# A fused attention and ternary-MLP kernel: the first batch normalised by VectorE, half of the first keys issued by ScalarE, epsilon added by GpSimd

## What is computed

```python
x = x + jnp.tanh(g_xattn[0]) * xattn(_layernorm(x), ctx_512, ctx_512)     # 32 query heads, 8 key/value heads, D = 16
x = x + jnp.tanh(g_ffn[0]) * ffn(_layernorm(x), w_gate, w_up, w_down)

def _layernorm(x, eps=1e-05):
    return (x - mean(x)) / sqrt(var(x) + eps)

def h_bitlinear(x, w):                      # ternary weights, 8-bit activations
    xq = act_quant(fwht(x))                 # Walsh-Hadamard transform, then rounding per token
    return xq @ weight_quant(w).T

def ffn(h):
    return h_bitlinear(silu(h_bitlinear(h, w_gate)) * h_bitlinear(h, w_up), w_down)
```

## Time and profile before

| | us |
|---|---|
| median of 3 runs | 474.78 |
| lowest, highest | 474.51, 475.0 |
| the profiled execution, its own time | 474.27 |
| its span in the trace | 472.5 |
| what lies around the span | 1.77 |

### The profile page before, as it was taken

One profiled execution on the slowest core, in us unless ns is written; L12 is line 12 of the kernel. 1 busy time (PEld: TensorE's weight loads), 2 busy tenths in 40 slices (PEclk: granted clock), 3 DMA queues, 4 the chain that ended last, 5 costly groups with the idle time before them and its releaser, 6 DMA issues.

```text
span 472.5 us, 9016 instructions
## 1 busy us (share of the span) xinstructions
PE 458.6 (97%) x3130; PEld 298.9 (63%) x3130; DVE 391.0 (83%) x745; ACT 292.8 (62%) x465; POOL 211.8 (45%) x314
## 2 busy tenths in 40 slices
PE   8999999999999989999999999999999999999997
PEld 7665656566656534468944469864468874479664
DVE  4889998888977759859998967999895999889892
ACT  4478886667777688877647417643616663647460
POOL 4245455989888464655006734202916300930000
PEclk9999999999999999999999999999999999999999
DMA  7999120121014050000100651100361110153086
GB/s 223 323 348 347 45 53 12 24 58 25 13 22 112 13 166 36 1 1 13 24 11 1 112 135 32 22 11 0 67 141 61 24 24 0 28 92 61 1 140 217
DMA packets 68183, 35.90 MB, mean 76 GB/s; under 512 B 50288, under 2 KB 62960, under 8 KB 68144
## 3 DMA queue, kind: packets, MB, share of 16 engines
q1 hardware_dynamic: 67728, 34.61, 28.8%
q10 hardware_dynamic: 416, 0.79, 0.5%
HBM read 19.26 MB, written 4.19 MB: 50 GB/s over the span
## 4 chain that ended last, share of the span: by engine, by line
PE 70%; DVE 13%; issue 7%; ACT 4%; POOL 2%; DMA 1%; SPq 1%; DVEq 0%; POOLq 0%; ACTq 0%
PE ps L863 15%; PE ps L619 10%; PE ps L917 9%; PE ps L602 8%; PE ps L662 6%; PE ps L940 6%; PE ps L679 3%; PE ps L929 2%; PE ps L931 2%; PE ps L806 2%; DVE wst L1447 2%; ACT wst L1052 2%; DVE y_split L1422 2%; PE ps L716 1%; PE ps L627 1%
## 5 line engine op out<-in xcount | busy, mean ns | idle before, releaser
L863 PE MATMUL ps<-wst 128*128 128x512 bf16 x512 | 113.0, 379 | 2.1 <-DVE wst L1442 2.1
L1279 DVE TENSOR_REDUCE reg<-ps 128x4 f32<-128x512 f32 x128 | 81.9, 684 | 24.7 <-PE ps L619 24.0
L863 PEld LDWEIGHTS ps<-wst 128*128 128x128 bf16 x512 | 49.0, 98 | 62.2 <-DVE wst L1442 4.2
L619 PE MATMUL ps<-reg 32*128 32x256 f32 x512 | 86.7, 400 | 0.9 <-DMA reg<-in_k_t 0.5
L1014 ACT ACTIVATE reg<-ps 128x1024 f32<-128x1024 f32 x64 | 65.6, 1025 | 32.8 <-PE ps L627 32.5
L564 POOL TENSOR_TENSOR reg_rest<-reg_rest,z_sc 128x1024 f32<-128x1024 f32 x24 | 47.3, 2012 | 84.6 <-DVE z_sc L1484 84.6
L1146 ACT ACTIVATE wst<-wst 128x512 f32<-128x512 f32 x64 | 40.0, 627 | 51.8 <-DVE wst L1442 51.5
L917 PE MATMUL ps<-had_f,wst 128*128 128x128 f32 x512 | 67.1, 276 | 1.1 <-DVE wst L1447 1.1
L917 PEld LDWEIGHTS ps<-had_f,wst 128*128 128x128 f32 x512 | 64.1, 191 | 4.4 <-DVE wst L1447 1.8
L602 PE MATMUL ps<-reg 32*128 32x512 f32 x232 | 65.2, 639 | 0.0
L619 PEld LDWEIGHTS ps<-reg 32*128 32x128 f32 x512 | 58.7, 184 | 5.8 <-ACT reg L1036 1.0
(11 more groups left out here) (168 smaller groups left out, 738.1 us busy)
## 6 DMA issues: line engine op xcount, KB each, us to landing
wst<-in_w SPq DMA_DIRECT2D x16, 512.0 KB, 8.6
reg<-in_w SPq DMA_DIRECT2D x8, 512.0 KB, 5.6
out<-x_all SPq DMA_DIRECT2D x16, 256.0 KB, 2.1
x_all<-in_x SPq DMA_DIRECT2D x3, 1024.0 KB, 9.5
reg<-in_k_t SPq DMA_DIRECT2D x32, 32.0 KB, 2.4
reg<-in_v SPq DMA_DIRECT2D x4, 256.0 KB, 4.1
x_all<-in_x ACTq DMA_DIRECT2D x1, 512.0 KB, 4.8
reg_rest<-reg SPq DMA_TRANSPOSE x20, 3.0
```

What stands on the lines that cost most here:

```text
L619: last = pe.matmul(ps[:, row_banks(r) + m, 256 * g:256 * g + 256], q_t[n % 4][strip(i), P * h:P * h + P], kpad[n // CHUNK % 2][strip(i), n ...
L863: last = pe.matmul(ps[:, banks[ob % n], :], tern_gu[:, ob // 2, m, j, P * (ob % 2):P * (ob % 2) + P], q1_t[:, j, :], start=(j == 0), stop= ...
L1279: dve.tensor_reduce(neg_max[n % 2][:, g:g + 2, i + m, :], ps[:, row_banks(r) + m, :].rearrange("p (g a t) -> p g a t", g=2, a=2), AX_X, AL ...
```

## The change

It has three parts, and some bookkeeping.

1. The first batch is normalised by VectorE: `first_queries` adds epsilon, waits for GpSimd's power (`first_rsqrt`, which forms no `shift` for batch 0), and does subtract and multiply in one instruction with the strided read of `x_all`. ACT's `normalise_q(0)` goes. In VectorE's queue this stands ahead of `selectors` and `statistics_q(1)`.
2. The first keys of heads 4 to 7 are asked for by ACT, behind batch 1; SP asks for heads 0 to 3 only.
3. For all other batches epsilon is added by GpSimd: `statistics_q` and `statistics` end with `bn_aggr`, and `rsqrt_q`, `front_scale` and `front_scales` begin with a `tensor_scalar` add and a wait for its result.

The bookkeeping: the statistics buffer is doubled, small tiles are views of one tile `few`, semaphore counts follow, one of 16 `spin` calls at the start goes, and PE waits for `identb_set` and `sel_set` only where it first uses those tiles.

```diff
-            load_keys(0)
+            load_keys(0, range(NKV // 2))
@@ GpSimd
-            def rsqrt(n, ready, done, par): ...
+            def first_rsqrt():
+                pool.wait_ge(sem("ve_first"), 1)
+                pool.tensor_tensor(rstd[:, 0:1], ve[:, 0:1], mhalf[:, :], ALU.pow).then_inc(sem("rs_first"), 1)
 def rsqrt_q(n):
-                pool.wait_ge(sem("ve_done"), n + 1)
-                reach(pool, sem("qn_done"), min(n - 1, 4))
+                pool.wait_ge(sem("mv_done"), n + 1)
+                if n == 2:
+                    pool.wait_ge(sem("qn_first"), 1)
+                elif n > 2:
+                    pool.wait_ge(sem("qn_done"), min(n - 2, 3))
                 reach(pool, sem("qp_done"), n - 5)
+                pool.tensor_scalar(ve[:, par:par + 1], mv[:, par, 1:2], EPS, None, ALU.add).then_inc(sem("ve_done"), 1)
+                pool.wait_ge(sem("ve_done"), n)
 def front_scale(tb):
-                rsqrt(Index(None, tb), "f_ve", "f_rs", 2)
                 pool.wait_ge(sem("f_mv"), tb + 1)
+                pool.tensor_scalar(ve[:, 2:3], mv[:, 2, 1:2], EPS, None, ALU.add).then_inc(sem("f_ve"), 1)
+                pool.wait_ge(sem("f_ve"), tb + 1)
+                pool.tensor_tensor(rstd[:, 2:3], ve[:, 2:3], mhalf[:, :], ALU.pow).then_inc(sem("f_rs"), 1)
 def front_scales(u):
+                reach(pool, sem("f_mv"), u.times(UB, UB))
+                pool.tensor_scalar(ve[:, 2:2 + UB], mv[:, 2:2 + UB, 1], EPS, None, ALU.add).then_inc(sem("f_ve"), UB)
                 reach(pool, sem("f_ve"), u.times(UB, UB))
@@ PE
-            spin(16)
+            spin(15)
             pe.wait_ge(sem("ident_in"), 16)
-            pe.wait_ge(sem("identb_set"), 1)
-            pe.wait_ge(sem("sel_set"), 2)
@@ ScalarE
             act.dma_start(x_all[:, 1, :], x[1]).then_inc(sem("x_one"), 16)
+            act.wait_ge(sem("k_zero"), 1)
+            for kv in range(NKV // 2, NKV):
+                i = kv % 4
+                act.dma_start(kpad[0][32 * i + D:32 * i + 2 * D, :, 1, :],
+                              k_t.rearrange("(d k) (b t) -> k d b t", k=NKV, b=NB)[kv, :, 0:CHUNK, :]
+                              ).then_inc(sem("k_in0"), 16)
...
-            normalise_q(0)
@@ VectorE
 def statistics(n, par):
+                reach(dve, sem("f_mv"), n.times(1, -1))
+                dve.bn_stats(st_f[:, n.const % 2, :], x_all[:, n.times(1), :]).then_inc(sem("f_bn"), 1)
                 reach_apart(dve, sem("tanh_done"), (sem("f_bn"), n.times(1, 1)))
+                dve.bn_aggr(mv[:, par, :], st_f[:, n.const % 2, :]).then_inc(sem("f_mv"), 1)
-                dve.wait_ge(sem(names[1]), n.times(1, 1))
-                dve.tensor_scalar(ve[:, par:par + 1], mv[:, par, 1:2], EPS, None, ALU.add).then_inc(sem(names[2]), 1)
+            def first_queries():
+                dve.wait_ge(sem("mv_done"), 1)
+                dve.tensor_scalar(ve[:, 0:1], mv[:, 0, 1:2], EPS, None, ALU.add).then_inc(sem("ve_first"), 1)
+                dve.wait_ge(sem("rs_first"), 1)
+                dve.tensor_scalar(q_norm[0].rearrange("p (m a d) -> p m a d", a=2, d=D),
+                                  x_all[:, 0, :].rearrange("p (d a m) -> p m a d", d=D, a=2),
+                                  mv[:, 0, 0:1], rstd[:, 0:1], ALU.subtract, ALU.mult).then_inc(sem("qn_first"), 1)
...
             statistics_q(0)
+            first_queries()
             selectors()
             statistics_q(1)
```

More of the change, by code:

```diff
@@ L168, in flamingo_block @@
         t8m = sb("t8m", [P, T8], F32)
-        st = sb("st", [P, 6], F32)
         mv = sb("mv", [P, 2 + UB, 2], F32)
@@ L173, in flamingo_block @@
         shift = sb("shift", [P, 2 + UB], F32)
-        mhalf = sb("mhalf", [P, 1], F32)
         r_sum = sb("r_sum", [P, 2, HALF], F32)
-        tg = sb("tg", [P, 2], F32)
-        graw = sb("graw", [P, 2], F32)
-        part = sb("part", [P, 2 * NCH], F32)
[L179 to L184, removed]
+        few = sb("few", [P, 41], F32)
+        tg, graw, mhalf = few[:, 0:2], few[:, 2:4], few[:, 4:5]
+        wsum, wsc, w_inv = few[:, 5:8], few[:, 8:11], few[:, 11:14]
+        wsd_tg, magics = few[:, 14:15], few[:, 15:17]
+        st, st_f = (few[:, k:k + 12].rearrange("p (n k) -> p n k", n=2) for k in (17, 29))
+        m_magic, p_magic = magics[:, 0:1], magics[:, 1:2]
+        part = sb("part", [P, 2 * NCH], F32)
         f_max = sb("f_max", [P, 8], F32)
@@ L268, in _, with load_keys @@
         def _(sp):
-            def load_keys(c):
-                for kv in range(NKV):
+            def load_keys(c, heads=range(NKV)):
+                for kv in heads:
                     i, a = kv % 4, kv // 4
@@ L416, in normalise_q @@
                 par = n % 2
-                pool.wait_ge(sem("sh_done"), n + 1)
+                pool.wait_ge(sem("sh_done"), n)
                 reach(pool, sem("tq_done"), n - 1)
@@ L514, in step @@
                     early_scales(EARLY_HAD[b])
-            rsqrt_q(0)
+            first_rsqrt()
             rsqrt_q(1)
@@ L605, in quarter @@
                         pe.wait_ge(sem("mt_done"), 1)
+                        pe.wait_ge(sem("sel_set"), 2)
                         for m, i in enumerate(own):
@@ L694, in turn_max @@
                 pe.wait_ge(sem("ms"), 5 * n + 5)
+                if n == 0:
+                    pe.wait_ge(sem("identb_set"), 1)
                 if n > 0:
@@ L705, in turn_queries @@
                     return
-                pe.wait_ge(sem("qn_done") if n < 4 else sem("qp_done"), n + 1 if n < 4 else n - 3)
+                if n == 0:
+                    pe.wait_ge(sem("qn_first"), 1)
+                else:
+                    pe.wait_ge(sem("qn_done") if n < 4 else sem("qp_done"), n if n < 4 else n - 3)
                 if n == 3:
@@ L1058, in normalise_q @@
                 par = n % 2
-                act.wait_ge(sem("sh_done"), n + 1)
+                act.wait_ge(sem("sh_done"), n)
                 reach(act, sem("tq_done"), n - 1)
@@ L1238, in selectors, with statistics @@
                     dve.tensor_copy(sel[:, a, :], sel_of[:, a:a + 1].broadcast_to([P, P])).then_inc(sem("sel_set"), 1)
[L1240 to L1244, removed]
-                dve.wait_ge(sem(names[1]), n.times(1, 1))
-                dve.tensor_scalar(ve[:, par:par + 1], mv[:, par, 1:2], EPS, None, ALU.add).then_inc(sem(names[2]), 1)
[L1248 to L1251, removed]
+            def statistics(n, par):
+                reach(dve, sem("f_mv"), n.times(1, -1))
+                dve.bn_stats(st_f[:, n.const % 2, :], x_all[:, n.times(1), :]).then_inc(sem("f_bn"), 1)
+                reach_apart(dve, sem("tanh_done"), (sem("f_bn"), n.times(1, 1)))
+                dve.bn_aggr(mv[:, par, :], st_f[:, n.const % 2, :]).then_inc(sem("f_mv"), 1)
[6 more added lines that the diff above has]
+                                  mv[:, 0, 0:1], rstd[:, 0:1], ALU.subtract, ALU.mult).then_inc(sem("qn_first"), 1)
             def statistics_q(n):
@@ L1262, in statistics_q @@
                 par = n % 2
-                reach(dve, sem("sh_done"), n - 1)
-                dve.bn_stats(st[:, :], x_all[:, n, :]).then_inc(sem("bn_done"), 1)
+                if n == 2:
+                    dve.wait_ge(sem("qn_first"), 1)
+                reach(dve, sem("sh_done"), n - 2)
+                reach(dve, sem("mv_done"), n - 1)
+                dve.bn_stats(st[:, n % 2, :], x_all[:, n, :]).then_inc(sem("bn_done"), 1)
                 dve.wait_ge(sem("bn_done"), n + 1)
-                dve.bn_aggr(mv[:, par, :], st[:, :]).then_inc(sem("mv_done"), 1)
-                dve.wait_ge(sem("mv_done"), n + 1)
-                dve.tensor_scalar(ve[:, par:par + 1], mv[:, par, 1:2], EPS, None, ALU.add).then_inc(sem("ve_done"), 1)
+                dve.bn_aggr(mv[:, par, :], st[:, n % 2, :]).then_inc(sem("mv_done"), 1)
             def maximum(n, k):
@@ L1321, in step @@
                     reach(dve, sem("f_ap"), FRONTS[b])
-                    statistics(Index(None, FRONTS[b]), ("f_bn", "f_mv", "f_ve"), 2)
+                    statistics(Index(None, FRONTS[b]), 2)
             def early_peak(tb):
@@ L1384, in front_statistics @@
                         dve.wait_ge(sem("f_s4"), u.times(2, -2))
-                statistics(n, ("f_bn", "f_mv", "f_ve"), 2 + tb)
+                statistics(n, 2 + tb)
             def input_peak(n, bank=1):
```

2 lines of the change are left out of this document (1 added, 1 removed).

## The result

| | us |
|---|---|
| before, median of 6 runs | 474.70 (474.29 to 475.0) |
| after, median of 6 runs | 472.72 (472.43 to 472.95) |
| ratio, with its 95% interval | 0.9961 (0.9951 to 0.9971) |
| profiled executions, before and after | 474.27 and 472.9 |
| their spans | 472.5 and 471.1 |

The changed kernel is 1.98 us faster; 0.17 was forecast, and the range began at 473.2. A repeat on another chip gave 472.73 against 474.49, 1.76 us less.

What follows compares the result with a forecast made beforehand. PE, busy 458.6 of 472.5 us, was taken to bound the kernel, with a latency at its start. Terms -1.05 + 0.78 - 0.2 + 0.3 = -0.17 us, from the median 474.78, gave 474.6; range 473.2 to 475.7.

Steps and rivals of the forecast that it cites:

- The start: Before PE's first score row: split keys and VectorE's normalisation bring it from 9.71 to 8.66 us, -1.05 us.
- the estimate of 0.9 us: First normalisation: alternative length of VectorE's strided instruction by the page's factor, making the start 0.16 us better.
- What is behind the start: Batch 1's later mean and later-issued batches 2 and 3 stay covered, so PE loses nothing: counted at 0.
- The cover of 0.8 us: Batches 2 and 3: landing at 10.2 us, wanted by VectorE at 11.0, so 0.8 us to spare.
- Rival 2: Batches 2 and 3 land at 13.1 us, VectorE holds row maxima, PE loses 1.4 us: 476.0 us, chance 0.07.
- Steps: Attention steps: GpSimd's added epsilon work makes PE wait 0.39 us at two of four early turns, +0.78 us.
- The lateness of GpSimd: Attention steps: the add and wait in `front_scale` and `rsqrt_q` delay GpSimd by 0.50 us (0.16 + 0.34).
- the forecast's wait at the early turn: PE idle about 0.4 us ahead of L725 in steps 9 and 11, none in 7 and 13.
- a sign of being wrong: Attention steps: the prediction called itself wrong if PE never waits at L725; 0.39 us per wait was forecast.
- End of attention: Two `statistics` and their `ve` instructions in the chain, 0.15 us each, half hidden: -0.2 us for both.
- Boundaries: Two loop boundaries: last `ve` goes (-0.2), GpSimd adds 0.23 and 0.10; +0.15 us each, +0.3 for two.
- Rival 1: GpSimd's addition is hidden, PE doesn't wait at L725, boundaries come out even: 473.5 us, chance 0.26.

Runs made afterwards that it cites:

- s_start: The changed kernel with epsilon added by VectorE for all batches but the first; 471.65 us against 474.21 for the kernel before.
- k_keys: The kernel before with only the first keys split over two queues, SP and ACT; 473.84 us against 474.21 for the kernel before.
- p_split: The changed kernel with one 128x2 VectorE scale instruction in `early_peak` split into two of 128x1; 472.45 us against 474.49 for the kernel before.
- e_steps: The changed kernel with epsilon on GpSimd in the attention steps, on VectorE for the units' scales; 473.61 us against 474.49 for the kernel before.

## Why the prediction was wrong, point by point

**The start, -1.05 forecast.** The mechanism was right: the keys alone moved the first row by 0.47 us (0.44 forecast), both together by 1.25 us in the profiled pair. Two sizes were off. VectorE's strided instruction was taken at 1.06 us by adding GpSimd's penalty for the stride; it takes 0.72, only 0.13 over the contiguous row. Part of that isn't seen, since PE now ends its warm-up matmuls at about 7.1. The Trainium skill's rule of the 16-byte lines (SBUF — State Buffer, Door 1: The DMA port swizzle), weighed there against the move, does little to VectorE in this case (0.13 us), and the estimate of 0.9 us there was too long as well. And one execution's landing of the keys, 9.58 us, was taken for the typical one, though that execution was 0.51 us faster than the median; by the traces that we have this may hide an estimated 0.1 to 0.4 us of the gain (a typical first row at 9.85 or 10.06 in place of 9.71).

**What is behind the start, counted at 0.** Right for after in its amount: its VectorE waits 0.34 us for the third batch, and PE doesn't. The cover of 0.8 us wasn't there, though. ACT issued the transfer at 4.64 us and not at 5.4, but it took 6.6 us and not 4.8. In s_start's trace the wait is 0.68 us, and its lead shrinks from 1.51 to about 0.9 by the first steps. Rival 2 named the mechanism, at the wrong price: where the batch came late enough (k_keys, p_split), PE's idle time was followed by a stretch at half clock, and these executions took 478 to 480 us.

**Steps, +0.78 forecast.** They cost 1.07 us between turns 7 and 11, less 0.33 won before, so 0.74. That this is near 0.78 is luck. The lateness of GpSimd (0.50 forecast, 0.54 at L500 in step 8) was right, and the forecast's wait at the early turn appears in p_split, once. But in the changed kernel PE never waits there, which the prediction had named as a sign of being wrong; 0.71 of the 1.07 us goes through another wait, on VectorE, which the profile of before had already shown: a 128x2 instruction of 0.45 us next to 128x1 ones of 0.15. I read it as a slow instruction and not as a held one. The other 0.36 us is the open part, and the 0.33 won before wasn't forecast.

**End of attention, -0.2 forecast.** -0.42: the `ve` instruction wasn't only half hidden, and VectorE left the chain altogether.

**Boundaries, +0.3 forecast.** -0.52. This is the largest error, 0.8 us, and the step that failed is "each `statistics` gains a wait for the previous aggregate, so its pace stays". The wait is for `f_mv` to reach n - 1, which is the aggregate of two batches back, since the statistics buffer is now double. So the next statistics don't wait, the pace goes from 1.13 to 0.94 us, and four of them give GpSimd more than its add costs. e_steps, with `ve` back on VectorE in the units alone, has the old pace and none of this gain. The forecast also took PE's wait of 0.24 us for granted at both boundaries, and before's timeline has it only at the first.

The sum with the measured terms is -1.25 + 0.74 - 0.42 - 0.52 = -1.45 us, where the spans differ by 1.4; with the means of the first rows (10.06 and 8.38) in place of the pair's it would be -1.9, between the two medians' 1.76 and 1.98. That the keys' landing is what makes up the rest is likely and not shown.

Rival 1 came out nearest in time (473.5), for wrong reasons: GpSimd's addition wasn't hidden, PE paid for it through VectorE.

## What to carry to other kernels

Two latencies that end close together have to be shortened together, and a start that hangs on a transfer has to be read from several executions, not from one. Before an instruction is moved to GpSimd, look at what VectorE does beside GpSimd's long instructions: where, as here, a small VectorE instruction of more than one column takes longer than its like and ends together with a GpSimd one, suspect that it was held, so that a delay of GpSimd becomes a delay of VectorE. When a wait counts a semaphore, work out which instance it names before calling it a dependence on the last one.

## What the runs showed of the hardware that I had not expected

- A VectorE `tensor_scalar` of 128x512 floats that reads SBUF with a step of 128 bytes took 0.72 us; the same pattern takes 1.244 on GpSimd and 1.26 on ACT.
- One VectorE instruction of 128x1024 took 0.68 or 2.25 us, depending on where in a gapless row of 2 us GpSimd instructions it started (9.2 or 9.4 us behind the row's start): about 1 us of the total time hangs on it, in a place that no edit touched.
- TensorE's clock fell to half after 1.64 us of idle time near 9 us of the kernel in one trace, and stayed there for some 17 us; 4 of 12 executions of that kernel were of this kind, and none of 12 with the idle time filled by matmuls down to 0.67. In another trace 1.60 us of idle time near 10 us left the clock at full speed.
